# Two spectral layers on a 45 x 90 image: inverse rows read one step earlier, two more row buffers at the end, and another order of two products

## The reference

```
f = fft2(x, axes=(1, 2), norm='ortho')                 # layer 0
Xk = (f.real - f.imag)[:, :, :46] in 8 blocks of 48, rows 0:45, columns 0:23
o1 = relu(Xk @ w1[0] + b1[0]);  o2 = o1 @ w2[0] + b2[0]
y = ifft2(softshrink(o2, 0.01) padded with zeros).real + x
xf = rfft2(y)                                          # layer 1
complex two-layer network with relu and softshrink on rows 0:45, columns 0:23
out = irfft2(...) + y
```

## Time and profile before

| | |
|---|---|
| median of 3 executions | 567.0 us |
| profiled execution, its own time | 569.88 us |
| its span, first to last instruction | 568.1 us |
| mean granted TensorE clock | 0.965 of full |
| TensorE matmul busy | 512.1 us, 90% of the span |
| VectorE, ScalarE, GpSimd busy | 306.2, 211.1, 135.6 us |
| DMA traffic | 104.60 MB, mean 184 GB/s |
| SyncE's queue: share of the 16 DMA engines | 37.9% |
| GpSimd's queue: share of the 16 DMA engines | 27.2% |

### The profile page before, as it was taken

How to read it: one execution, slowest core, us unless ns; L and a number is a source line. 1 busy time by engine, 2 the same in 40 slices (tenths; PEclk the granted TensorE clock), 3 DMA queues, 4 the chain that set the end, 5 groups by cost and what they waited for, 6 DMA issues and landing times.

```text
span 568.1 us, 14234 instructions
## 1 busy us (share of the span) xinstructions
PE 512.1 (90%) x5824; PEld 376.1 (66%) x5824; DVE 306.2 (54%) x675; ACT 211.1 (37%) x473; POOL 135.6 (24%) x146
## 2 busy tenths in 40 slices
PE   4379999989998999989999899989999899999863
PEld 1157777757776777767776677767777577887531
DVE  6324455346754676436754477446763376556543
ACT  0015444533344433534344333544245323343201
POOL 9611111112320232102330133211331111111124
PEclk9859999989999999989999999999999899999879
DMA  8779663486886788686885887776886855373387
GB/s 190 242 179 261 179 166 85 105 196 172 245 221 147 191 217 233 175 181 178 242 217 143 193 204 241 198 172 179 254 200 163 191 145 154 99 149 100 101 224 234
DMA packets 76717, 104.60 MB, mean 184 GB/s; under 512 B 7761, under 2 KB 63303, under 8 KB 76526
## 3 DMA queue, kind: packets, MB, share of 16 engines
q1 hardware_dynamic: 57622, 55.97, 37.9%
q0 software_dynamic: 10608, 40.45, 27.2%
q10 hardware_dynamic: 8424, 7.28, 4.9%
HBM read 52.23 MB, written 51.43 MB: 182 GB/s over the span
## 4 chain that ended last, share of the span: by engine, by line
PE 77%; DMA 8%; DVE 5%; POOL 2%; SPq 2%; ACT 2%; issue 2%; POOLq 0%; ACTq 0%; DVEq 0%
PE ps L653 14%; PE ps L586 13%; PE ps L679 12%; PE ps L556 9%; PE ps L640 9%; PE ps L599 7%; PE ps L617 7%; DMA jr<-scr_i 4%; PE ps L666 4%; PE ps L628 3%; SPq L275 2%; DVE img L535 2%; DMA scr_f<-fs 2%; DVE ns L509 1%; POOL img L369 1%
## 5 line engine op out<-in xcount | busy, mean ns | idle before, releaser
L586 PE MATMUL ps<-jr,cst 64*128 64x384 f32 (+1 forms) x368 | 87.5, 543 | 22.0 <-DMA jr<-scr_i 15.4
L535 DVE TENSOR_TENSOR img<-ps,img 90x768 f32<-90x768 f32 x92 | 82.8, 900 | 40.2 <-PE ps L586 36.0
L352 POOL TENSOR_TENSOR xs<-xs,nt 128x360 f32<-128x360 f32 (+1 forms) x48 | 41.4, 863 | 212.0 <-DVE nt L487 135.5
L653 PE MATMUL ps<-wt,o 128*109 128x96 f32 (+1 forms) x768 | 85.4, 263 | 0.4 <-issue 0.2
L653 PEld LDWEIGHTS ps<-wt,o 128*109 128x109 f32 (+1 forms) x768 | 76.4, 171 | 13.6 <-issue 12.9
L509 DVE SCALAR_TENSOR_TENSOR ns<-p,ps 109x384 f32<-109x384 f32 x96 | 53.1, 553 | 57.5 <-ACT p L425 57.5
L556 PE MATMUL ps<-img,cst 128*64 128x384 f32 (+1 forms) x368 | 72.1, 506 | 13.1 <-DMA img<-x 7.7
L361 POOL DMA_DIRECT2D y<-img x42 | 34.7, 827 | 190.3 <-DVE img L535 190.3
L599 PEld LDWEIGHTS ps<-cst,bt 128*64 128x64 f32 x1472 | 63.2, 141 | 20.4 <-issue 13.9
L418 ACT ACTIVATE o<-ps,wt 97x180 f32<-97x180 f32 (+1 forms) x96 | 33.8, 406 | 111.2 <-PE ps L640 111.2
L679 PE MATMUL ps<-ns,cst 64*90 64x192 f32 x736 | 74.6, 335 | 0.0
(11 more groups left out here) (41 smaller groups left out, 415.6 us busy)
## 6 DMA issues: line engine op xcount, KB each, us to landing
y<-img POOLq DMA_DIRECT2D x35, 540.0 KB, 5.4
img<-x POOLq DMA_DIRECT2D x30, 540.0 KB, 8.1
scr_i<-et SPq DMA_DIRECT2D x48, 270.0 KB, 4.3
scr_f<-fs SPq DMA_DIRECT2D x176, 72.0 KB, 2.0
bt<-scr_f SPq DMA_DIRECT2D x40, 270.0 KB, 3.9
jr<-scr_i SPq DMA_DIRECT2D x48, 216.0 KB, 5.3
img<-x ACTq DMA_DIRECT2D x10, 540.0 KB, 6.5
y<-img SPq DMA_DIRECT2D x11, 270.0 KB, 3.6
```

The source lines that it names most:

```text
L352: nc.gpsimd.tensor_tensor(re, re, nt[s % 2][:, :, 0:kws(s), 0:H], ALU.subtract).then_inc(re_ok, 1)
L535: nc.vector.tensor_tensor(y, p, y, ALU.add).then_inc(i_add, 1)
L586: last = mm(ps[:, B0 + r, 0:n], K["w_inv"][64 * r:64 * r + 64, :], jr[k][64 * r:64 * r + 64, at, 0:n], start=True, stop=True)
L653: last = mm(ps[0:rows, P2 + p, b * 2 * BS:(b + 1) * 2 * BS], o11[:, b, 2 * p:2 * p + kw, :].rearrange("p k m -> p (k m)")[:, 0:rows], w21[ ...
```

## The change

Four edits. (1) `rows` is listed in step i = 1 of a task instead of i = 2. (2) In every iteration s whose predecessor carried three inverse groups, `e` and `c1` change places; these are i = 4, 5, 0 and 1 behind the inverse of a task. (3) For the last task all five sets of rows are asked for at once: sets 3 and 4 go into `bt[0]` and `bt[1]`, which are free once the last `a` has been multiplied, with a semaphore each. (4) The requests of the last task at groups 2 and 5 go away.

```diff
-        if 0 < s <= NSTEPS:
-            order.append(("c1", s - 1))
-        order += inv[s][0:1]
-        if s > 1:
-            order.append(("e", s - 2))
-        order += inv[s][1:2]
+        c1 = [("c1", s - 1)] if 0 < s <= NSTEPS else []
+        e = [("e", s - 2)] if s > 1 else []
+        first, second = (e, c1) if s > 0 and len(inv[s - 1]) == 3 else (c1, e)
+        order += first + inv[s][0:1] + second + inv[s][1:2]
...
-        if i == 2 and 0 < t < TASKS:
+        if i == 1 and 0 < t < TASKS:
             order += [("rows", t - 1, j) for j in range(JR)]
...
-    order += [("rows", TASKS - 1, j) for j in range(JR)]
+    order += [("rows", TASKS - 1, j) for j in range(len(JSETS))]
...
+        j_tail = [sem(f"last_set{j}_loaded") for j in range(JR, len(JSETS))]
...
+        def set_rows(t, j):
+
+            if t == TASKS - 1 and j >= JR:
+                return bt[j - JR][:, 0:(JSETS[j][1] - JSETS[j][0]) * 2 * HC].rearrange("p (g c) -> p g c", c=2 * HC)
+            return jr[bank_of(t, j)[0]]
...
-                if kind == "rows" or (kind == "inv" and what[1] in (2, 5)):
+                if kind == "rows" or (kind == "inv" and what[0] < TASKS - 1 and what[1] in (2, 5)):
...
+                    if t == TASKS - 1 and j >= JR:
+                        sp.wait_ge(a_mm, 2 * NT)
+                    elif used:
                         m = t * len(JSETS) + j - JR
                         sp.wait_ge(i_mm, m // len(JSETS) * GROUPS + JSETS[m % len(JSETS)][1])
```

More of the change, by code:

```diff
@@ L295, in _ @@
                                  et[s % 2][0:2 * H, :, :]).then_inc(e_st[s % 2], 16)
-                if kind == "rows" or (kind == "inv" and what[1] in (2, 5)):
+                if kind == "rows" or (kind == "inv" and what[0] < TASKS - 1 and what[1] in (2, 5)):
                     t, j = what if kind == "rows" else (what[0], jset[what[1]] + JR)
                     k, used = bank_of(t, j)
+                    landed = j_tail[j - JR] if t == TASKS - 1 and j >= JR else j_ld[k]
                     if j == 0:
@@ L303, in _ @@
                         sp.wait_ge(j_clr, j + 1)
-                    if used:
+                    if t == TASKS - 1 and j >= JR:
+                        sp.wait_ge(a_mm, 2 * NT)
+                    elif used:
                         m = t * len(JSETS) + j - JR
@@ L309, in _ @@
                     if g0 == GROUPS - 1:
-                        sp.dma_start(jr[k][0:2 * KWP, 0, 0:HC], rows[:, 4 * g0, :]).then_inc(j_ld[k], 16)
+                        sp.dma_start(set_rows(t, j)[0:2 * KWP, 0, 0:HC], rows[:, 4 * g0, :]).then_inc(landed, 16)
                     else:
@@ L313, in _ @@
                         for r in range(2):
-                            sp.dma_start(jr[k][64 * r:64 * r + 2 * KWP, 0:g1 - g0, :], four[:, :, r, :]).then_inc(j_ld[k], 16)
+                            sp.dma_start(set_rows(t, j)[64 * r:64 * r + 2 * KWP, 0:g1 - g0, :], four[:, :, r, :]).then_inc(landed, 16)
                 if kind == "inv" and what[0] == TASKS - 1:
@@ L564, in _ @@
                     if g == JSETS[j][0]:
-                        pe.wait_ge(j_ld[k], rows_landed(t, j))
+                        if t == TASKS - 1 and j >= JR:
+                            pe.wait_ge(j_tail[j - JR], 16 * set_dmas(j))
+                        else:
+                            pe.wait_ge(j_ld[k], rows_landed(t, j))
                     at = g - JSETS[j][0]
@@ L585, in _ @@
                         n = min(2, h1 - h0 - 2 * r) * HC
-                        last = mm(ps[:, B0 + r, 0:n], K["w_inv"][64 * r:64 * r + 64, :], jr[k][64 * r:64 * r + 64, at, 0:n], start=True, stop=True)
+                        last = mm(ps[:, B0 + r, 0:n], K["w_inv"][64 * r:64 * r + 64, :], set_rows(t, j)[64 * r:64 * r + 64, at, 0:n], start=True, stop=True)
                     last.then_inc(i_mm, 1)
```

## The result

553.5 us (median of 4 executions, 552.79 to 554.8) against 570.63 us for the kernel before (4 executions, 566.54 to 577.86). The ratio is 0.9721, 95% interval 0.9676 to 0.9767: faster by 2.8%. The ratio is taken over the fast executions alone, which leaves out the one of 577.86 us, in a slower state of the chip. The forecast was 553.0. The median before is no firm mark: over 19 more executions it was 567.7 (565.7 to 575.4). Between the two profiled executions (569.88 and 552.87 us) 17.0 us went, where the forecast's sum had 15.1.

The account below looks back on a forecast made before the run. TensorE, 90% busy, was taken as the bound, stalled by late rows. Savings 13.1 + 4.6 - 3.6 + 1.0 = 15.1 us gave 554.8 from the profile or 551.9 from the median; forecast 553.0, range 548.5 to 558.5.

Parts of the forecast that it names:

- The stall: First inverse group of six tasks: TensorE's wait for rows goes when they are requested one step earlier, 13.1 us off.
- The clock: Three of the six stall places: the granted clock no longer falls once the stalls go, 4.6 us off.
- The exchange: `e` ahead of `c1` in 24 iterations: 1.3 us lost at i = 4, 5, 0 and 2.3 at i = 1, together 3.6.
- The tail: End of the last task: extra row buffers save 1.0 us, ends 0.2 and 1.5.
- The queue's term: SyncE's last stores: two row DMAs no longer pass among them, worth 1.0 us at 270 KB in 0.94 us.
- the chain's term: ScalarE and GpSimd adding four groups in turn in the tail: last addition ends 0.2 us earlier at best.
- Rival A: Forward stores stick behind the moved rows in SyncE's queue, 5 us lost a task, 583 us; chance 0.04.
- the rule: All issuing engines' DMAs interleave on 16 DMA engines: refill bytes delay forward stores an estimated 1.7 us; sum would stay.
- The request's wait for the store of `e`: SyncE's early rows request for set 0 waits for the previous task's last `e` store: 0, at most 1.2 us.
- the 2.9 us between profile and median: Median 567.0 lies 2.9 us below the profiled 569.9: clock falls, shorter stalls or the profile's burden; the middle was taken.

Follow-up runs that it names:

- edit 2 alone: Kernel before with only `e` put ahead of `c1` in the 24 iterations, rows still requested in step i = 2: 569.91 us, ratio 1.0035.
- edits 3 and 4 alone: Kernel before with only the two more row buffers for the last task: 567.9 us, ratio 0.9975.
- all but the exchange: Full change without the swap of `e` and `c1`: 551.99 us, ratio 0.9716.
- the two kernels with added products: Full change without the swap of `e` and `c1`, plus 16 or 4 small products at the start: 549.89 and 550.61 us.
- edit 1 alone: Kernel before with only the rows listed in step i = 1 instead of i = 2: 551.72 us, ratio 0.9722.
- the tail's stores: Full change without the `e`/`c1` swap, with three GpSimd groups in the last task and stores in the order the adds end: 551.77 us, ratio 0.9729.
- the doubled rows: Full change without the `e`/`c1` swap, with six same transfers repeated behind each early rows request (1.3 MB more): 571.56 us, ratio 1.0036.

## Why the prediction was right

**The stall** (-13.1 us). Right: six waits for rows, all gone, and asked for a step ahead. A later experiment adds that half the lead would do: the request at the head of i = 2 gave the same six distances. Its size was a little short: in the three waits without a fall of the clock the distance of step 3 is 0.27 us more than the idle time above 11.34, not the 0.16 that the sum took from one start to the next, which makes 12.1 + 6 x 0.27 = 13.7 us.

**The clock** (-4.6 us). Right in size for this profile: stall and clock together were put at 17.7 us and came to 18.3, of which 13.7 is the stall and 4.6 the clock. The link is now shown by a series of idle times in front of the first inverse group. 0 in the full change: no fall. 0.8 to 1.3 us: none in six. 1.8 to 2.6 us: three of six before, one of six with edit 2 alone, two of six with edits 3 and 4 alone. 4.3 to 4.6 us: six of six, and five of these longer. Behind 2 us the fall isn't certain and doesn't go by length alone: one followed 1.92 us and none followed 2.56. The sum took three falls, counted in the very profile that the comparison here uses; other executions may have had one or two more or fewer, at 1.5 us each. Over its executions the kernel before spreads over 10 us and more, and the longer ones have the lower mean clock (0.949 at 579.12 us, 0.976 at 565.15), the new one over 2 us in only four executions; that falls behind the waits make most of this is likely, but where the clock fell is known for the profiled executions alone.

**The exchange** (+3.6 us). Right in place and size: 0.40 us at i = 1 against 0.39 predicted, 0.08 and 0.01 against at most 0.07. The timeline of a step i = 1 after the change, to set beside the earlier trace rows:

```profile
343.74 1.34 PE L690 MATMUL ps<-ns,cst 64*90 64x192 f32 x11 [0.28 <-DVE ns L525]
...
347.37 1.61 PEld L664 LDWEIGHTS ps<-wt,o 128*109 128x109 f32 x16 [0.44 <-ACT o L426]
```

Both waits are the two that were named: `e` behind VectorE's additions, `d1` behind ScalarE's relu. In the times only 2.0 us (edit 2 alone) and 1.5 us (full change against all but the exchange) of the 3.4 showed. The gap without a releaser can hide the rest: it cost 3.4 us in the profile of all but the exchange, but 0.5 in that of the kernel before, and what it costs in executions without a profile isn't known. Against the two kernels with added products, which have neither the exchange nor the gap, the full change is 3.6 and 2.9 us slower by the medians, though in other rounds. The prediction had no term for the gap, which with a shorter one came to 0.6 us between the two profiles.

**The tail** (-1.0 us). The queue's term was right (0.9 us behind the last addition); the chain's term, at most 0.2 us for the better, was not. The number came out near by luck: in this pair of profiles the tail gave 1.5 us, and they came from the clock. Before, it fell to half in two places, in the last steps and in the last task's inverse. Two stretches of the kernel before, and then one of the kernel after:

```profile
528.00:531.00 3.00, 3.00 (x24) 2.28 (x22) 1.12 (x4) 0.64 (x2) 0.00 (x0) 0.53 0.01 5
543.00:551.00 8.00, 5.23 (x18) 2.46 (x17) 2.95 (x4) 0.00 (x0) 1.62 (x2) 0.64 0.95 236
```

```profile
526.00:534.00 8.00, 5.23 (x17) 2.31 (x15) 2.62 (x4) 0.00 (x0) 1.62 (x2) 0.61 0.94 237
```

The first fall is gone after the change, and up to the last `t` that gained 1.5 us. Nothing ties that to an edit: the last distance is 7.64 us with edit 1 alone too, 9.19 or 9.20 in four of the 14 profiles (before, edit 2 alone, edits 3 and 4 alone, the tail's stores) and 7.6 in the other ten. The second fall is in both kernels and about 3 us longer after the change, so that ScalarE's second copy for GpSimd had to wait for TensorE, not for GpSimd as before:

```profile
538.44 0.81 ACT L447 ACTIVATE p<-ps 90x768 f32<-90x768 f32 x1 [2.71 <-PE ps L597]
```

So the last addition ended 27.9 us after the last `t` (546.73 - 518.84), before 26.95, and the 0.9 us of the queue went there. From the last `t` but one to the end it is 39.9 us against 41.4.

**Rival A and the rule.** The stores behind the rows were slow to land, 6.3 us where the median of all `fs` stores is 2.4. ScalarE's wait, new against before, and the landing of the four stores issued from 356.2 us on:

```profile
ACT fs L399 <- DMA scr_f<-fs: 2.8, 2, 1.5
```

```profile
scr_f<-fs SPq DMA_DIRECT2D x4, 72.0 KB, 6.3
```

The copies waited up to 1.5 us, which the prediction didn't expect, and it cost TensorE nothing (distances of 10.25 and, in step 3, 11.34). There is spare time, and the doubled rows show what is beyond it. That the issuing engines' transfers interleave (the Trainium skill, "DMA: Bandwidth & Descriptors", section "Issuing engines are not separate DMA queues") didn't get to matter: the stores behind the rows took 6.3 us where they had taken 5.7 before, and no run here shows the interleaving by itself.

**Smaller misses.** The request's wait for the store of `e` was put at 1.2 us at most; one was 2.8 (SyncE, four waits of 3.9 us in sum), with no effect. And the 2.9 us between profile and median were no property of the profile: 569.9 lies inside the spread of the kernel before. Halving it was a guess that happened to land well: 553.0 is 0.5 us from the measured median, while the sum was 1.9 us short of the 17.0 between the two profiles, by 0.6 in the stall, 0.2 in the exchange, 0.6 in gaps that had no term and 0.5 in the tail. The saving from the later median of 19 executions, 567.7 - 15.1 = 552.6, would have come to about the same as the forecast.

## What to carry to other kernels

Where a wait of 2 us stands in front of a full matmul engine, price the slow clock behind it too, and expect it behind some waits and not behind others. Here waits longer by 2.4 us (2.0 to 4.4) cost 4 us more each (3.05 to 7.0), and waits shorter by 0.9 us saved 1.7 each. Read back how early a transfer has to be asked for and move it by that: half a step was enough here. And count an exchange of two products by who waits for each when nothing lies between: this one cost 0.4 us where no inverse group stood between them and brought nothing anywhere.

## What was not expected of the hardware

TensorE stopped for 0.2 to 2.8 us in the middle of one run of products, released by nothing in the profile, at one of two fixed places of the program or at both, in the profiles of nine kernels of 14; 16 or 64 more instructions at the start were followed by profiles without it and by the lowest medians, 550.6 and 549.9 us. A stop can cost more than its length: one of 1.6 us was followed by a granted clock of 0.76 and 0.67 in two stretches of 3 us and lengthened its step by 3.4 us, the one of 2.8 us lengthened it by 5.9.
